# Softmax reciprocals of three attention layers moved from VectorE to GpSimd as a power, with loads and preparations reordered

## The reference

```python
q = layernorm(x); k = v = ctx              # [16, 64, 256]
# per batch: 8 heads of 8 tokens; each head is an 8 x 256 block, and the
# "positions" that attend to one another are its 256 columns
if n == 1: q, k = q / |q|, k / |k|         # norm over the 8 rows of a head
s = q_head.T @ k_head * scale              # 256 x 256 per batch and head
p = softmax(s)                             # layers 0 and 2 subtract the row maximum
x = x + (v_head @ p.T)                     # layer 2: times gamma
```

## Time and profile before

| | us |
|---|---|
| median of 3 runs | 1515.39 (1515.09 to 1521.4) |
| the profiled execution: its own time | 1514.85 |
| its span, first to last instruction | 1513.1 |
| PE busy | 1158.9 (77%) |
| DVE busy | 681.9 (45%) |
| ACT busy | 626.3 (41%) |
| POOL busy | 520.8 (34%) |
| mean granted TensorE clock | 0.851 of full |

### The profile page before, as it was taken

The page is one execution under the profiler, slowest core; times in us unless marked ns, Lnnn a source line. Parts: engine busy times, 40 slices in busy tenths (PEclk is TensorE's granted clock), DMA queues, the critical chain, the costliest instruction groups (busy, mean ns, idle before and its releaser), DMA issues. The chain is left out here.

```text
span 1513.1 us, 19093 instructions
## 1 busy us (share of the span) xinstructions
PE 1158.9 (77%) x6690; PEld 811.0 (54%) x6690; DVE 681.9 (45%) x1368; ACT 626.3 (41%) x981; POOL 520.8 (34%) x554
## 2 busy tenths in 40 slices
PE   1756855346885999186784999999996747999998
PEld 0423423133444887043343788888863426888886
DVE  6534648842115333563564533333346764333333
ACT  3424445625672443144362333433327333343432
POOL 3001123100012664111222566666641032666563
PEclk9967776666886999577695999999997877999999
DMA  6542122033511431333111243533310002333331
GB/s 192 136 142 82 33 68 90 24 100 102 144 50 32 133 110 50 118 85 95 55 45 40 88 121 99 175 107 112 110 43 8 1 22 67 120 111 107 114 105 66
DMA packets 61532, 132.33 MB, mean 87 GB/s; under 512 B 8781, under 2 KB 31949, under 8 KB 57352
## 3 DMA queue, kind: packets, MB, share of 16 engines
q1 hardware_dynamic: 61472, 131.56, 29.0%
HBM read 115.49 MB, written 15.45 MB: 87 GB/s over the span
## 5 line engine op out<-in xcount | busy, mean ns | idle before, releaser
L1151 POOL TENSOR_TENSOR f_hid<-f_gated,f_coef 128x512 f32<-128x512 f32 x152 | 224.1, 1475 | 169.6 <-DVE f_gated L1182 158.4
L1182 DVE TENSOR_TENSOR f_gated<-f_act_g,f_p_u 128x512 f32<-128x512 f32 x152 | 104.4, 688 | 271.5 <-PE f_p_u L1014 264.9
L730 DVE TENSOR_REDUCE a_maxes<-a_p_max 128x2 f32<-128x512 f32 x256 | 159.5, 679 | 92.8 <-PE a_p_max L552 92.8
L652 ACT ACTIVATE a_probs<-a_p_sc 128x1024 f32<-128x1024 f32 x192 | 186.2, 1017 | 31.4 <-PE a_p_sc L584 26.3
L552 PE MATMUL a_p_max<-a_k,a_q 72*128 72x256 bf16 x512 | 109.2, 343 | 105.3 <-DVE a_maxes L730 43.0
L1091 ACT ACTIVATE f_hid_hi<-f_hid 128x512 fp32r<-128x512 f32 x152 | 96.0, 632 | 208.6 <-POOL f_hid L1151 208.5
L1186 DVE TENSOR_TENSOR f_hid_lo<-f_hid,f_hid_hi 128x512 fp32r<-128x512 f32 x152 | 106.1, 698 | 150.5 <-ACT f_hid_hi L1091 150.1
L1086 ACT ACTIVATE f_act_g<-f_p_g 128x512 f32<-128x512 f32 x152 | 90.8, 598 | 168.5 <-PE f_p_g L1014 168.5
L584 PE MATMUL a_p_sc<-a_q,a_k 75*128 75x256 bf16 (+1 forms) x768 | 132.9, 308 | 33.8 <-ACT a_probs L652 25.5
L552 PEld LDWEIGHTS a_p_max<-a_k,a_q 72*128 72x128 bf16 x512 | 48.6, 114 | 156.4 <-DVE a_maxes L730 66.5
L603 PE MATMUL a_p_out<-a_probs,all_v 128*32 128x256 f32 x1536 | 126.2, 469 | 4.8 <-ACT a_probs L652 4.8
(11 more groups left out here) (273 smaller groups left out, 1857.1 us busy)
## 6 DMA issues: line engine op xcount, KB each, us to landing
f_w<-in_w SPq DMA_DIRECT2D x76, 384.0 KB, 3.5
f_coef<-coef SPq DMA_DIRECT2D x51, 512.0 KB, 3.7
a_q<-q_parts SPq DMA_DIRECT2D x24, 576.0 KB
a_k<-k_plain SPq DMA_DIRECT2D x48, 192.0 KB
outs<-a_out SPq DMA_DIRECT2D x48, 128.0 KB, 2.2
a_whole<-outs SPq DMA_DIRECT2D x48, 128.0 KB, 2.6
a_k<-k_unit SPq DMA_DIRECT2D x24, 192.0 KB
all_v<-in_v SPq DMA_DIRECT2D x4, 1024.0 KB, 9.2
```

Of the source, the lines that this page charges most:

```text
L652: nc.scalar.activation(probs[b % 2][:, 2 * pair:2 * pair + 2, :, :].rearrange("p h t d -> p h (t d)"), p_sc[pair % 2][:], ACT.Exp, scale=s ...
L730: nc.vector.tensor_reduce(maxes[b % 3][:, :, h], p_max[:, n % 3, :].rearrange("p (t d) -> p t d", t=NK), axis=AX.X, op=ALU.max, negate=Tru ...
L1151: nc.gpsimd.tensor_tensor(hid[c][:], gated[c][:], coef[slot(t, 2)][:, c * 512:(c + 1) * 512], ALU.mult).then_inc(hid_done, 1)
L1182: nc.vector.tensor_tensor(gated[c][:], act_g[c][:], p_u[c][:], ALU.mult).then_inc(gated_done, 1)
```

## The change: what it does

1. **Reciprocal.** `invert` and its 48 DVE instructions are gone. `add_tile` on POOL computes `y = sum ** -1` (`ALU.pow` with a tensor of -1), then one Newton step `2y - sum*y*y` in four passes of 128 x 256, then multiplies and adds as before. In layers 0 and 2 it stands behind `split_max(b + 2)` of odd b = 5, 7, ..., 15, one step later than before.
2. **Layer 1's keys** are prepared in layer 0's attention from a second copy of the context with a head per partition (`ctx_heads`, 1 MB): ACT squares and takes the root, DVE sums and inverts, and POOL scales and splits one of eight slices in each of steps 3 to 10, five passes of 128 x 256. The first feed-forward stage only stores them, in 24 DMAs. `gather` and `spread` are loaded in layer 1.
3. **Layer 0's loads.** The first load of values stands behind the stores of the second group, the others in steps 0, 4 and 6; `ident` and `gamma` come behind the first two query and key tiles; the rows of ones are one DMA.
4. **Layers 1 and 2** load only key tile 0 ahead of the stores, the others next to their query tile.
5. **Layer 1's preparation** interleaves the two normalizations, moves the split of groups 1 and 2 from ACT to POOL, and PE does three of the four `spread_out` behind step 0.

```diff
     def add_tile(i):
         w = whole[i % 2]
-        pool.wait_ge(inv_done, 2 * (i + 1))
+        pool.wait_ge(whole_loaded[i % 2], 32 * (i // 2 + 1))
         if i >= 1:
             pool.wait_ge(added, i)
+        minus_b = bass.AP(minus[:].tensor, minus[:].offset, [list(minus[:].ap[0]), [0, D]])
+        tt(inv[:], w[:, 1, :], minus_b, ALU.pow).then_inc(inv_done, 1)
+        pool.wait_ge(inv_done, 5 * i + 1)
+        tt(prod[:], w[:, 1, :], inv[:], ALU.mult).then_inc(inv_done, 1)
+        pool.wait_ge(inv_done, 5 * i + 2)
+        tt(prod[:], prod[:], inv[:], ALU.mult).then_inc(inv_done, 1)
+        pool.wait_ge(inv_done, 5 * i + 3)
+        tt(inv[:], inv[:], inv[:], ALU.add).then_inc(inv_done, 1)
+        pool.wait_ge(inv_done, 5 * i + 4)
+        tt(inv[:], inv[:], prod[:], ALU.subtract).then_inc(inv_done, 1)
+        pool.wait_ge(inv_done, 5 * i + 5)
         tt(prod[:], w[:, 0, :], inv[:], ALU.mult).then_inc(divided, 1)
...
     for b in range(B):
         if with_max and b + 2 < B:
             split_max(b + 2)
-        if b >= 4 and b % 2 == 0:
+        if b >= 5 and b % 2 == 1:
             add_tile(b // 2 - 2)
+        if layer == 0 and 3 <= b < 3 + CH:
+            if b == 3:
+                wait_keys(pool)
+            for what in range(5):
+                unit_keys.split(pool, one, what, b - 3)
...
     if with_max:
         for n in range(B * HEADS):
             take_max(n)
-            step, h = divmod(n - AHEAD, HEADS)
-            if step >= 4 and step % 2 == 0 and h in (2, 6):
-                invert(step // 2 - 2, h // 4)
-                n_inv = step // 2 - 1
-    for i in range(n_inv, NI):
-        for side in range(2):
-            invert(i, side)
...
     if layer == 0:
         dve.wait_ge(ident_loaded, 32)
         nc.vector.tensor_copy(m.ident_bf[:], m.ident[:]).then_inc(ident_ready, 1)
+        unit_keys.sums(dve)
+        unit_keys.invert(dve)
...
+    def sums(self, dve):
+        dve.wait_ge(self.squared, 1)
+        self.nc.vector.tensor_reduce(self.length[:], self.square.rearrange("p c d -> p d c"), axis=AX.X,
+                                     op=ALU.add).then_inc(self.summed, 1)
...
     if layer == 1:
         unit.squares(tt, 0)
+        norm.statistics(dve, link, 1)
         unit.clamp(dve, 0)
+        norm.finish(dve, link, 1)
         unit.invert(dve, 0)
         unit.scale(dve, 0)
+        unit.squares(tt, 1)
```

More of the change, by code:

```diff
@@ L312, in root @@
     def root(self, act):
-        self.norm.root(act, 0)
+        act.wait_ge(self.clamped, 1)
+        self.nc.scalar.activation(self.length[:], self.length[:], ACT.Sqrt).then_inc(self.root_ready, 1)
     def invert(self, dve):
-        self.norm.invert(dve, 0)
-    def spread_out(self, pe, n):
-        self.norm.spread_out(pe, n)
-    def scale(self, dve, n):
-        self.norm.scale(dve, n)
-    def split(self, pool, n, ones):
-        tt, p = self.nc.gpsimd.tensor_tensor, self.parts
-        t = p.tiles(n)
-        one = bass.AP(ones[:].tensor, ones[:].offset, [list(ones[:].ap[0]), [0, 2], [0, D]])
-        pool.wait_ge(self.norm.out_ready, n + 1)
-        tt(p.part[:, 0, t, :], self.keys[:, t, :], one, ALU.mult).then_inc(p.hi_ready, 1)
-        p.take_high(pool, tt, n)
-        pool.wait_ge(p.rest_ready, n + 1)
-        tt(p.part[:, 1, t, :], self.keys[:, t, :], one, ALU.mult).then_inc(p.mid_ready, 1)
-        p.take_mid(pool, tt, n)
@@ L336, in store, with split @@
-    def store(self, sp, n):
-        for part in range(3):
-            self.parts.store(sp, part, n)
-    def wait_stored(self, sp):
-        for n in range(4):
-            self.parts.wait_stored(sp, n)
+        dve.wait_ge(self.root_ready, 1)
+        self.nc.vector.reciprocal(self.inverse[:], self.length[:]).then_inc(self.inverse_ready, 1)
+    def split(self, pool, one, what, c):
+        tt, part, src = self.nc.gpsimd.tensor_tensor, self.m.unit_part, self.keys[:, c, :]
+        one_b = bass.AP(one[:].tensor, one[:].offset, [list(one[:].ap[0]), [0, D]])
+        if what == 0:
+            pool.wait_ge(self.inverse_ready, 1)
+            tt(src, src, self.inverse[:], ALU.mult).then_inc(self.scaled, 1)
+        elif what == 1:
+            pool.wait_ge(self.scaled, c + 1)
+            tt(part[:, 0, c, :], src, one_b, ALU.mult).then_inc(self.hi_ready, 1)
+        elif what == 2:
+            pool.wait_ge(self.hi_ready, c + 1)
+            tt(src, src, part[:, 0, c, :], ALU.subtract).then_inc(self.rest_ready, 1)
+        elif what == 3:
+            pool.wait_ge(self.rest_ready, c + 1)
+            tt(part[:, 1, c, :], src, one_b, ALU.mult).then_inc(self.mid_ready, 1)
+        else:
+            pool.wait_ge(self.mid_ready, c + 1)
+            tt(part[:, 2, c, :], src, part[:, 1, c, :], ALU.subtract).then_inc(self.lo_ready, 1)
@@ L519, in _ @@
                         load_neg(b + 2)
-                    if b == 0:
-                        if layer == 0:
-                            for part in range(3):
-                                key_parts.store(sp, part, 2)
+                    if b == 0 and layer == 0:
+                        for part in range(3):
+                            key_parts.store(sp, part, 2)
+                        load_v(1)
                     if b == 1:
@@ L612, in _ @@
                     unit.gather(pe, 1)
-                    for n in range(1, 4):
-                        unit.spread_out(pe, n)
                 n_max = n_turn = 0
@@ L636, in _ @@
                             weigh(b - 1, "wxyz".index(what), n_turn)
+                    if layer == 1 and b == 0:
+                        for n in range(1, 4):
+                            unit.spread_out(pe, n)
                 for quarter in range(4):
@@ L1430, in _ @@
                 def _(sp):
-                    unit.load(sp, a)
                     for n in range(2):
                         sp.dma_start(raw[n][:], a[f"ternary{n}"]).then_inc(loaded[n], 16)
-                    for n in range(4):
-                        unit.store(sp, n)
-                    unit.wait_stored(sp)
+                    store_unit_keys(sp, m, unit_stored)
+                    sp.wait_ge(unit_stored, 3 * CH * 16)
                 @block.gpsimd
@@ L1440, in _ @@
                     nc.gpsimd.memset(ones[:], 1.0).then_inc(ones_set, 1)
-                    pool.wait_ge(unit.loaded, 16)
-                    unit.squares()
-                    pool.wait_ge(ones_set, 1)
-                    for n in range(4):
-                        unit.split(pool, n, ones)
                 @block.tensor
                 def _(pe):
-                    unit.gather(pe)
-                    pe.wait_ge(unit.clamped, 1)
                     pe.wait_ge(ones_set, 1)
@@ L1529, in _ @@
                     ternary(0, w1)
-                    unit.invert(dve)
                     dve.wait_ge(squared, NI)
```

249 lines of the change are left out of this document (144 added, 105 removed).

## The result

The changed kernel takes 2406.24 us (median of 4 runs, 2401.8 to 2408.85), the kernel before 1518.01 in the same comparison: ratio 1.585, 95% interval 1.580 to 1.590. The forecast was 1492 us with a range of 1445 to 1640; both were wrong.

The account below looks back on a forecast made before the run. PE was held to be bound by DVE's waits for `whole` tiles, the slow clock behind them and step 3's wait for ACT; −12 − 0.7 − 7.5 + 16 − 13 − 8.5 + 3 = −22.7 from 1514.85 gave 1492 us, 80% range 1445 to 1640.

Parts of the forecast that it names:

- The price of the power, p = 3.0 us: POOL's power on 128 x 256 takes 3.0 us, from DVE's reciprocal at 4.2 plain passes; 0.72 and 17 us as bounds.
- The slope, 14 us for each us: Whole kernel: each us of the power's price adds 8 us (eight stops) and 6 us (three tails).
- Eight stops: First and third attention: POOL's tile work beyond a 5.05 us window delays the split and PE behind steps 5, 7, 9, 11.
- The six tails: Ends of the three attentions: two runs of POOL's tile work follow at each, +5.3 us per layer, +16 in all.
- the rival: Whole kernel: the power is a plain pass of 0.72 us on POOL, sum −56, 1459 us; chance 0.17.
- First attention, start, −12: Layer 0: with 2 MB of values fewer ahead of its store, step 3 ends at about 80 instead of 92.09 us.
- The loops: Ten steps behind step 3: layer 0 from 106.7 to 106.0 us (−0.7), layer 2 from 102.7 to 95.2 (−7.5).
- First feed-forward stage, −13: Without POOL's key work and DVE's reciprocal and scalings, 4 us gained at the front and 9 in the loop.
- Layer 2's start, −8.5: Third attention: DVE's 9.81 us wait for tiles shrinks, with fewer key tiles and DMAs ahead; bounds 0 to −9.8 us.
- Layer 1, +3: Second attention's start: PE's part shrinks, but masks load now and step 3's copy waits for SP; bounds −8 to +5 us.
- The late transfer: Loops of layers 0 and 2: `whole` tiles still land late, POOL waits, loops gain nothing; 1512 us; chance 0.10.
- The slow power: POOL's power costs far more than DVE's reciprocal: 1618 us at 10 us, about 1790 at 17; chance 0.38.

Follow-up runs that it names:

- sections 1, 2, 6: 1: changed kernel, power replaced by a product, 1457.68 us; 2: powers timed alone on kernel before, 41.24 us; 6: kernel before, later place, POOL's power, 2328.65 us.
- section 4: Changed kernel with the power on 32 or 128 of 256 columns and a plain pass on the rest: 1571.37 us (ratio 1.039) and 1927.84 us (1.276).
- plain-pass kernel: Changed kernel with the power replaced by a product of the same operands, so the sums are not inverted: 1457.68 us, ratio 0.962.
- section 7: Changed kernel with reciprocals back on DVE one step later, identity and gamma loaded ahead of the context's second copy: 1435.61 us, ratio 0.947.

## Why the prediction was wrong

**The price of the power, p = 3.0 us.** This step failed, and everything else is small beside it. The value was taken from DVE's reciprocal (4.2 plain passes); measured are 41.13 us, 57 passes (sections 1, 2, 6). The upper bound of 17 us, 24 passes for a logarithm and an exponential, was an invention about how the operation is made; no row spoke for 24, so it was no bound. The other estimate beside it, 2.6 us more than a plain pass, was short by a factor of 15 (40.4 measured). The row chosen as nearest was one of another engine, and the text itself said that no row bounds the price from above. The sign turns at about 3.4 us, not 4.6, an estimate (the plain pass leaves 57 us, at the 20.8 per us of section 4).

**The slope, 14 us for each us.** Eight stops were right in number and size: behind step 5 the forecast's rule gives 5.6 + 40.4 + 4.0 − 5.05 = 45.0 us, and 44.2 are measured; in the third attention 41.8 against 40.1 to 41.3. (The forecast's own sum for layer 2 has A = 8.6 where its terms give 8.7.) The six tails were wrong. The tiles of steps 13 and 15 have no split behind them and stood in the text as free, but they pile up: four runs follow PE's last transpose (section 4), and on an eighth of the columns the end of the first attention and the whole of the second grew by 19.1 us each, the end of the third by 18.9, 3.5 powers and not two. Eight stops and 3 × 3.5 make 18.5; most of the rest of 20.8 is the clock behind stops that become long (in the third attention the steps behind them take 8.7 to 9.5 us where they took 6.15). At 20.5 and at 40.5 us all 24 powers stand on the path, save 22 to 23 us in all.

**The other terms** can be read from the plain-pass kernel, for which the rival gave 1459 us (1457.68 measured). That agreement holds errors that cancel:

| | 1st attention | 1st FFN | 2nd attention | 3rd attention | sum |
|---|---|---|---|---|---|
| rival's terms | −22.7 | −13 | +5.3 | −25.2 | −55.6 |
| measured (spans) | −17.1 | −15.3 | +13.2 | −38.1 | −57.3 |

- *First attention, start, −12.* In the changed kernel step 3 ends at 95.11, not at 80: it came 3 us later than before, not 12 sooner. DVE's wait for gamma was missed; I had written "till about 29" for a load that landed at 38.2. The stop at step 3 fell from 12.97 to 5.81, as forecast (about 6). With gamma early (section 7) the step still ends at 87.92, so the gain would have been 4.
- *The loops.* −0.7 and −7.5 at p = 3; at the plain pass −13 and −19 were forecast, −21.9 and −34.2 measured. The rule for the stops gave 4.6 and 1.35 where 2.6 to 3.7 and 0.80 came. The reductions, left as they were, take 685 ns (679 before). The charge of 3.3 us of slow clock per short stop was wrong for stops of 0.8 us, which bring none.
- *The tail* with a plain pass, +2.3: in the first attention 24.35 us behind the last transpose against 24.0, in the third 26.7 against 24.9, so +0.4 and +1.8.
- *First feed-forward stage, −13:* −15.1. The cause named is there (DVE's passes take 0.29 us); how much each part of it brings was not measured.
- *Layer 2's start, −8.5:* step 3 ends 70.1 us into the stage, 77.6 before: −7.5 (71.8 with the plain pass: −5.8).
- *Layer 1, +3:* +13.2. PE waits 9.8 us for the masks where it waited 6.2 for DVE, the preparation is 8.1 us longer since the spread products wait behind step 0, and PE then stands 21.4 us behind the late store of batch 0, a stop that the kernel before does not have. Which part the clock has in it is open.

**The rivals.** The late transfer (1512 us) fell: with a plain pass POOL, asking at the new place, waits for no whole tile in the loops of layers 0 and 2, and first for 1.99 us at 193.90, in the tail. The slow power was the right one in kind, and held 0.38, the largest of the four; its figures of 1618 and about 1790 were for 10 and for 17 us, and by its own slopes (8 + 6 + 8 for each us) the second is 1772.

## What to carry to other kernels

An operation that no row of the trace shows on its engine has no upper bound from a row of another engine: time it by itself first, one instruction is enough. On an engine with a window between its turns, what exceeds the window is paid at every turn, and what is queued behind the last turn piles up and is paid too, however free its place looks. When a small edit moves a stage by more or less than its own rows say, look at the granted clock of that stage before giving the difference a cause. The gain sought here, no wait of DVE for its transfer, came from asking one step later, not from moving the operation to another engine.
